# Projections from x laid out transposed, attention groups written out, and the causal mask of the probabilities made by GpSimd

## What is computed

```
q = (x @ wq).reshape(b, s, 32, 32)      # 32 heads of 32
k = (x @ wk).reshape(b, s, 8, 32)       # 8 key heads, each for 4 query heads
v = (x @ wv).reshape(b, s, 8, 32)
scores = einsum('bihd,bjhd->bhij', q, k) * SCALE
scores = where(tril, scores, min)
attn = softmax(scores)
out = einsum('bhij,bjhd->bihd', attn, v) @ wo
x = layernorm(x + out)
...
```

## Time and profile before

| | |
|---|---|
| median of 3 runs | 3816.9 us (3811.1 to 3820.51) |
| the profiled execution | 3811.96 us, span 3810.2 us |
| busy in the span | PE 3600.9 (95%), PEld 2489.0, DVE 1987.4 (52%), ACT 1453.1 (38%), POOL 1561.2 (41%) |
| granted PE clock | 0.977 of full in the mean |
| costliest lines | POOL L552 1331.6 us, DVE L726 1357.6, ACT L688 1032.1, PE L582 919.9, PE L606 716.4, PE L616 584.1 (with v) |

### The profile page before, as it was taken

How to read it: one execution, slowest core, us unless ns; L and a number is a source line. 1 busy time by engine, 2 the same in 40 slices (tenths; PEclk the granted TensorE clock), 3 DMA queues, 4 the chain that set the end, 5 groups by cost and what they waited for, 6 DMA issues and landing times. The chain is left out here.

```text
span 3810.2 us, 74380 instructions
## 1 busy us (share of the span) xinstructions
PE 3600.9 (95%) x26773; PEld 2489.0 (65%) x26773; DVE 1987.4 (52%) x3597; ACT 1453.1 (38%) x1821; POOL 1561.2 (41%) x678
## 2 busy tenths in 40 slices
PE   8999998999999999999999999999769999999965
PEld 7888885565565566566565655665358888888841
DVE  3121116766566666666666666666243444444458
ACT  2111112555555555555555555555520111111124
POOL 0000001867777687678678777866400000000000
PEclk9999997999999999999999999999879999999989
DMA  5333325011111111111211111100153222222236
GB/s 191 108 108 124 105 90 114 22 50 46 40 33 50 49 34 40 47 46 29 51 46 33 40 47 45 32 25 10 48 137 83 76 79 82 78 83 74 64 129 246
DMA packets 222648, 269.67 MB, mean 71 GB/s; under 512 B 59608, under 2 KB 145112, under 8 KB 222328
## 3 DMA queue, kind: packets, MB, share of 16 engines
q1 hardware_dynamic: 222328, 265.50, 23.8%
HBM read 167.38 MB, written 97.52 MB: 70 GB/s over the span
## 5 line engine op out<-in xcount | busy, mean ns | idle before, releaser
L726 DVE TENSOR_REDUCE p_part_max<-p_qm 128x1 f32<-128x512 f32 (+3 forms) x2240 | 1357.6, 669 | 727.5 <-PE p_qm L582 457.9
L552 POOL TENSOR_TENSOR p_psums<-p_psums,p_probs 128x1024 f32<-128x1024 f32 x560 | 1331.6, 2378 | 49.3 <-ACT p_probs L688 2.2
L688 ACT ACTIVATE p_probs<-p_km 128x1024 f32<-128x1024 f32 x1024 | 1032.1, 1024 | 555.7 <-PE p_km L606 438.5
L582 PE MATMUL p_qm<-p_k_st,p_q_st 96*128 96x512 f32 (+3 forms) x2560 | 919.9, 422 | 14.8 <-DMA p_q_st<-q_hi 10.7
L606 PE MATMUL p_km<-p_q_st,p_k_st 97*128 97x512 f32 x2048 | 716.4, 429 | 30.7 <-issue 20.8
L582 PEld LDWEIGHTS p_qm<-p_k_st,p_q_st 96*128 96x128 f32 x2560 | 497.1, 197 | 228.9 <-DVE p_part_max L726 161.2
L32 POOL MEMSET p_ident<- 128x128 f32 x4 | 0.8, 204 | 1518.7 <-POOLq L799 928.8
L616 PE MATMUL p_o<-p_probs,p_v 128*32 128x256 f32 (+1 forms) x9216 | 584.1, 373 | 0.0
L606 PEld LDWEIGHTS p_km<-p_q_st,p_k_st 97*128 97x128 f32 x2048 | 356.7, 192 | 176.2 <-issue 131.8
L548 POOL TENSOR_TENSOR p_psums<-p_probs 128x1024 f32<-128x1024 f32 x95 | 226.4, 2383 | 546.6 <-ACT p_probs L688 546.6
L616 PEld LDWEIGHTS p_o<-p_probs,p_v 128*32 128x32 f32 x9216 | 271.3, 110 | 217.9 <-issue 62.6
(11 more groups left out here) (153 smaller groups left out, 4051.1 us busy)
## 6 DMA issues: line engine op xcount, KB each, us to landing
p_q_st<-q_hi SPq DMA_DIRECT2D x128, 256.0 KB, 4.5
p_x_raw<-in_L_attn_x SPq DMA_DIRECT2D x8, 2048.0 KB, 8.3
q_hi<-p_out_hi SPq DMA_DIRECT2D x64, 256.0 KB, 2.0
q_lo<-p_out_lo SPq DMA_DIRECT2D x64, 256.0 KB, 2.3
p_q_st<-q_lo SPq DMA_DIRECT2D x64, 256.0 KB, 4.4
attended_T<-p_o_raw SPq DMA_DIRECT2D x128, 128.0 KB
p_a_raw<-attended_T SPq DMA_DIRECT2D x32, 512.0 KB, 4.3
p_recip<-reciprocals SPq DMA_DIRECT2D x128, 128.0 KB, 5.8
```

Of the source, the lines that this page charges most:

```text
L552: pool.tensor_tensor(sums[:, :, :], sums[:, :, :], probs[s % PB][:, :, :], ALU.add).then_inc(added, 1)
L582: last = pe.matmul(bank[:, x * keys:(x + 1) * keys], q_st[par][0:ROWS, c, h + x, sub * P:(sub + 1) * P], k_st[par][0:ROWS, j * CK:j * CK + ...
L688: act.activation(probs[s % PB][:, :, :].rearrange("p h q -> p (h q)"), km[s % 2][:, :, :].rearrange("p a b -> p (a b)"), ACT.Exp, scale=SC ...
L726: dve.reduce_max(part_max[c][:, h:h + heads, sub, j], qm[bank_of(i)][:, 0:item_width(i)].rearrange("p (h k) -> p h k", h=heads), AX.X).the ...
```

## The change

**Projections.** The kernel gets a second input, x transposed on the host (`in_xT`, 1024 x 4096). `x_raw` is loaded as it is needed, in 8 chunks of 128 rows of it, each with a semaphore of its own, and ACT and DVE split it straight from SBUF. The transposes, the identity and the four PSUM banks for them are gone; `acc` has seven banks, and the first tile opens seven groups at once. The weights come through three buffers instead of two. The first x chunk is issued ahead of the first weights; the load of chunk k of tile t + 2 waits for the split of the same chunk of tile t + 1.

**Attention, loops.** All 16 groups are written out on every engine; registers and the empty semaphore increments (`hold`) are gone.

**Attention, mask.** `mask_k` and its products L609 and L601 are gone. Instead POOL sets to zero, in `probs`, what lies above the diagonal: one selection of 128 x 4 x 128 for each of the steps t = 2c and t = 2c + 1, behind the adds of the same chunk. PE waits for both selections before it takes the values of a chunk's last slot. The items' mask (L585) stays.

```diff
-    GB = 4
-    TB = 4
+    GB = 7
+    WB = 3
...
-            def load_x(t):
-                sp.dma_start(x_raw[:, :, :], x_t[t, :, :, :]).then_inc(x_in, 16)
+            def load_x(t, k):
+                sp.dma_start(x_raw[:, k, :], xT[k * P:(k + 1) * P, bass.ds(t * TT, TT)]).then_inc(x_in[k], 16)
...
-                    if g == T_AT + KC - 1 and load:
-                        sp.wait_ge(transposed, (t + 2) * KC)
-                        load_x(t + 2)
-
-            load_w(0)
-            load_x(0)
-            for k in range(1, KC):
+                    if T_AT < g <= T_AT + KC and load:
+                        sp.wait_ge(xT_lo_done, (t + 1) * KC + g - T_AT)
+                        load_x(t + 2, g - T_AT - 1)
+
+            for k in range(KC):
+                load_x(0, k)
                 load_w(k)
-            sp.wait_ge(transposed, KC)
-            load_x(1)
+            for k in range(KC):
+                sp.wait_ge(xT_lo_done, k + 1)
+                load_x(1, k)
...
-                for s in range(SUB):
-                    last = pe.transpose(tp[k % TB][:, s * P:(s + 1) * P], x_raw[:, s, k * P:(k + 1) * P],
-                                        ident[:, :])
-                last.then_inc(transposed, 1)
...
-                act.wait_ge(transposed, t * KC + k + 1)
-                act.activation(xT_hi[par][:, k, :], tp[k % TB][:, :], ACT.Copy).then_inc(xT_hi_done, 1)
+                act.wait_ge(x_in[k], 16 * t + 16)
+                act.activation(xT_hi[par][:, k, :], x_raw[:, k, :], ACT.Copy).then_inc(xT_hi_done, 1)
...
+            def select(n, s):
+
+                c, t = STEPS[s]
+                pool.wait_ge(exp_done, n * NS + s + 1)
+                part = probs[s % PB][:, :, (t - 2 * c) * P:(t - 2 * c + 1) * P]
+                pool.affine_select(out=part, in_=part, compare_op=ALU.is_ge, fill=0.0, base=0,
+                                   pattern=[[0, REP], [1, P]], channel_multiplier=-1).then_inc(selected, 1)
 
             def group(n, plan):
...
+                for s, (c, t) in enumerate(STEPS):
+                    if 1 <= t < plan.pooled[c]:
+                        add(n, plan, s)
+                    elif t >= 2 * c:
+                        select(n, s)
 
             group(0, SUMS)
-            with pool.Fori(0, NG // 2 - 1) as i:
-                group(2 * i + 1, SUMS)
-                group(2 * i + 2, SUMS)
+            for n in range(1, NG - 1):
+                group(n, SUMS)
...
-                    pe.matmul(four, keys, q_st[par][0:ROWS + 1, c // 2, :, q0 + P:q0 + CQ], start=True, stop=False)
-                    last = pe.matmul(four, ident_bf[:, :], mask_k[:, :].unsqueeze(1).to_broadcast([P, REP, P]),
-                                     start=False, stop=True)
+                    last = pe.matmul(four, keys, q_st[par][0:ROWS + 1, c // 2, :, q0 + P:q0 + CQ], start=True, stop=True)
...
-                                         start=True, stop=t < 2 * c)
-                        if t == 2 * c:
-                            last = pe.matmul(two[:, :, 0:P], ident_bf[:, :],
-                                             mask_k[:, :].unsqueeze(1).to_broadcast([P, 2, P]), start=False, stop=True)
+                                         start=True, stop=True)
...
                 pe.wait_ge(exp_done, n * NS + steps[-1] + 1)
+                if STEPS[steps[-1]][1] == 2 * c + 1:
+                    pe.wait_ge(selected, 2 * (n * NC + c + 1))
...
-            with pe.Fori(0, NG // 2 - 1) as i:
-                group(2 * i + 1, 1, STEADY)
-                group(2 * i + 2, 0, STEADY)
+            for n in range(1, NG - 1):
+                group(n, n % 2, STEADY)
```

More of the change, by code:

```diff
@@ L153, in _, with product @@
         def _(pe):
[L154 to L158, removed]
[L159 to L166 removed]
+            def product(par, g, k):
+                xh, xl, bank = xT_hi[par], xT_lo[par], acc[g % GB]
                 if g < QG + KG:
@@ L173, in product, with tile @@
                                w_hi[:, k, D + KV:WC], w_lo[:, k, D + KV:WC], k == 0, k == KC - 1)
-            def tile(t, par, begin=0, last=False):
+            def tile(t, par, begin=0):
                 pe.wait_ge(xT_lo_done, (t + 1) * KC)
                 for g in range(begin, G):
-                    if not (isinstance(t, int) and t * G + g < GB):
-                        pe.wait_ge(evacuated, t * G + g + 1 - GB)
+                    pe.wait_ge(evacuated, t * G + g + 1 - GB)
                     for k in range(KC):
-                        done = product(t, par, g, k)
+                        done = product(par, g, k)
                     done.then_inc(group_done, 1)
[L183 to L188, removed]
             for k in range(KC):
-                if k + 1 < KC:
-                    transpose_chunk(0, k + 1)
                 pe.wait_ge(w_lo_done, k + 1)
@@ L194, in _ @@
                 for g in range(GB):
-                    done = product(0, 0, g, k)
+                    done = product(0, g, k)
                     if k == KC - 1:
@@ L201, in _ @@
                 tile(2 * i + 2, 0)
-            tile(NT - 1, 1, last=True)
+            tile(NT - 1, 1)
         @block.scalar
@@ L466, in group @@
                 before = batch_head(n - 1)
-                started = not (isinstance(n, int) and n == 0)
+                started = n > 0
                 events = []
@@ L515, in _ @@
             group(0, 0, OPENING)
-            with sp.Fori(0, NG // 2 - 2) as i:
-                group(2 * i + 1, 1, STEADY)
-                group(2 * i + 2, 0, STEADY)
-            group(NG - 3, 1, STEADY)
+            for n in range(1, NG - 2):
+                group(n, n % 2, STEADY)
             group(NG - 2, 0, STEADY, load=False)
@@ new lines, in add @@
+            def add(n, plan, s):
+                c, t = STEPS[s]
+                sums = psums[c % 2]
+                pool.wait_ge(exp_done, n * NS + s + 1)
+                if t == 1:
+                    at_least(pool, chunk_done, n * NCHUNK + max(0, plan.chunks[c] - 1))
+                    pool.tensor_tensor(sums[:, :, :], probs[(s - 1) % PB][:, :, :], probs[s % PB][:, :, :],
+                                       ALU.add).then_inc(added, 1)
+                else:
+                    pool.wait_ge(added, n * NADD + plan.adds_through(s) - 1)
+                    pool.tensor_tensor(sums[:, :, :], sums[:, :, :], probs[s % PB][:, :, :],
+                                       ALU.add).then_inc(added, 1)
@@ L645, in group @@
                         values(n, par, sl - 1, plan)
-                    elif not (isinstance(n, int) and n == 0):
+                    elif n > 0:
                         values(n - 1, 1 - par, NSL - 1, SUMS)
             pe.wait_ge(ident_done, 2)
-            pe.wait_ge(consts_done, 6)
+            pe.wait_ge(consts_done, 5)
             for i in range(FIRST_AHEAD):
@@ L710, in _ @@
             group(0, OPENING)
-            with act.Fori(0, NG // 2 - 1) as i:
-                group(2 * i + 1, STEADY)
-                group(2 * i + 2, STEADY)
+            for n in range(1, NG - 1):
+                group(n, STEADY)
             group(NG - 1, CLOSING, LAST_SUMS)
@@ L741, in _ @@
             group(0, OPENING)
-            with dve.Fori(0, NG // 2 - 1) as i:
-                group(2 * i + 1, STEADY)
-                group(2 * i + 2, STEADY)
+            for n in range(1, NG - 1):
+                group(n, STEADY)
             group(NG - 1, CLOSING)
```

93 lines of the change are left out of this document (31 added, 62 removed).

## The result

The changed kernel takes 3840.8 us (median of 4 runs, 3839.7 to 3844.1) against 3815.5 for the kernel before: ratio 1.0067, interval 1.0050 to 1.0085, so it is slower by 0.7%. The prediction was 3850. The span of the profiled execution is 3838.0 us, 27.8 longer than before; 25.3 lie between the medians.

The account below looks back on a forecast made before the run. PE was taken to bound projections and attention. Gains 35.6 + 58.2 + 33.9 = 127.7 against losses 128.5 + 33 = 161.5, net +33.8 us, gave 3850 us, slower by 0.9%; 8 in 10 range 3785 to 3885.

Parts of the forecast that it names:

- Projections, 35.6: Projection stage: removing transposes gains 30.9 us and an earlier start of products 4.7, together 35.6 us.
- Edges, 33.9: Attention, groups 1 to 14 written out: six loop back edges go, 20.8 us idle and 13.1 slower PE, 33.9 gained.
- Masks, 58.2: Attention: mask products leave PE, priced by spacing at 3.64 us a group, 58.2 us gained; bounds nothing and 127.
- Waits, 128.5: Attention, chunks 6 and 7: PE waits for POOL's selections, 8.8 us a group, 5.3 in group 0, 128.5 lost.
- Clock, 33: Attention: PE comes back at a lower clock behind 15 waits, 2.2 us each, 33 us lost; bounds nothing and 51.
- Rival A: POOL's chain in attention is short enough: selections 0.5 us, waits 86.5, no clock loss, 3776 us, faster; chance 0.24.
- Rival B: Attention: the wait for POOL comes but PE's clock holds, 33 us less, 3817 us, no change; chance 0.14.
- Rival C: Attention: selections take 1.17 us, adding 19 us, and longer clock loss 18: 3887 us; chance 0.16 together with D.
- D: Attention: masks or edges are worth less than priced, up to 40 us slower; counted into C, together 0.16.

Follow-up runs that it names:

- masks on PE: The changed kernel with the mask products back on PE and no selections on POOL: 3762.2 us, ratio 0.9871.
- the best version: The changed kernel with two adds of chunk 7 fewer and the selections of chunks 6 and 7 ahead of the chunk's last add: 3729.5 us, ratio 0.9773.

## Why the prediction was right, and where it was not

The time (3840.8 for 3850), the sign and the mechanism were right; two terms were too large by nearly the same amount, on opposite sides.

- **Projections, 35.6:** 37.0 (first exponential 602.2 before, 565.2 now). Products start at 10.42 (I said 10.9).
- **Edges, 33.9:** their idle and low clock went. In the kernel before PE was idle for 20.8 us at them and busy at half clock for 28.9 us behind them, 14.5 lost: 35 us, near the price. Written out alone, groups 1 to 14 took 14.1 us less (1833.6), with 16.0 of waits on sums against it; of the 4 us that are left, 1.7 are a spell of 3.4 us at half clock from 1361.7. But in the changed kernel the gain is only on paper, since the loop's edges would have lain in the same wait. The ledger can carry it only together with the whole wait.
- **Masks, 58.2: the step that failed.** 30.1 measured. "I price them by spacing: 0.227 us for 512 columns, half for 256" took every product as bound by its columns. Here a mask of 512 columns behind its score product cost some 0.05 us and one of 256 0.08, so the truth lies midway between the price and the lower bound I had named, nothing. The Trainium skill ("TensorE: Matmul & The Clock Gate", section "Wait — 56ns, not 53.3ns?") gives back-to-back products of 512 columns 215.7 ns from start to start; for these products the runs disagree. What bounds them was not tested.
- **Waits, 128.5:** 99.4, or 6.9 us a group for 8.8, and 3.3 for 5.3 in group 0. Of the 1.9, 1.2 is the chain (57.6 us for 58.8): two selections take 1.18 us from the first's start to the next add, not 1.7. A selection lasts 0.633 us, and the second starts 0.59 behind the first. 0.7 is PE, which reached the slot later, since three chunks' masks had held it for 0.7 instead of 1.4. The page "GPSIMD Engine Reference" of the Trainium skill (section 3.1) gave 769 ns for 512 elements in a tight loop; measured is less than that, too.
- **Clock, 33:** 30, from the 59.3 us at half clock.

With these the sum is 99.4 + 30 - 37.0 - 30.1 - 33.9 = +28.4, for 27.8 between the profiled spans. The agreement of the forecast is therefore part luck: masks 28 too dear, waits 29 too dear.

Rival A (POOL in time, 3776) was nearer on POOL than the forecast: a selection every 0.59 us (it said 0.5, the forecast 0.85) and waits of 99.4 us (86.5 against 128.5). What sank it are the clock, which it put at nothing and which took 30 us, the masks at half their price (28) and the 13 us of waits above its own. Rival B (the clock holds, 3817) fell to the half clock at every wait. Rival C (1.17 us a selection, 3887) fell to the 0.633. D was true as a mechanism (a mask is worth half, 28 us less), but the shorter waits hid it: 10 of their 29 us come from the same fact, 0.7 us a group, the rest from cheaper selections.

## What to carry to other kernels

Before an engine is given work, follow its chain through the stretch where it has no hole: it was 54 us long there with 0.1 to spare, though the engine was idle for a quarter of the stage. Work shed by the bounding engine then also makes that chain late sooner. And take a wait away whole: cut to half, it gave 6 us, since the low clock behind it grew. With two adds fewer and four selections moved nothing waited, and that gave 111 us.

## What was not expected of the hardware

- A wait of 3.1 us on PE cost as much as one of 6.1, within 0.3 us a group: 10.2 us at half clock on busy products behind the one, 3.8 behind the other. Behind the 14 waits of 1.1 us on the sums the clock held (masks on PE). That is no safe length: PE is idle for 1.15 us once in every group anyway, and in the best version the clock fell to half for 3.4 us 3 us after PE had fallen idle in one of these (at 923.7).
- A 128x256 bf16 product accumulating behind a score product costs 0.08 us of PE, against a record of 0.28.
- The same loop in attention had 20.8 us of idle at its edges with one code of the projections and 35.7 with another; why is open.
- Three steps more of products with ones cost about 1.3 us of PE a group by an estimate (129.0, less the 136.5 - 6.1 - 0.8 - 1.9 = 127.7 of the changed kernel without its waits and low clock), where records of 0.61 us had made it 1.8. With the masks on PE it was 1.1: 130.8 us without a wait for 130.8 with one of 1.1.
